# Cross-attention mix from split float32r operands, with new rings and queue orders, in a one-core post-norm decoder layer

## Chip, cores and metric

One core of one Trainium2 chip runs the whole layer. The metric is the device time of one execution in microseconds (us). Before the change it is 554.73 us, the median of three runs (554.62 to 554.76).

## The reference

The input x has 8 sequences of 112 tokens and 1024 features, the context 8 x 375 tokens x 1024. All is float32.

```python
x = layernorm(x + self_attention(x))        # 16 heads of 64, rotary, causal; Wq, Wk, Wv, Wo of 1024x1024
a = einsum('bqd,bkd->bqk', x, ctx)          # cross-attention, one head of 1024 features
e = softmax(a, axis=-1)
c = einsum('bqk,bkd->bqd', e, ctx)          # the "mix"
x = layernorm(x + c)
y = x @ weight.T + bias + lora(x)           # 1024x1024; adapters of rank 16, by batch
x = layernorm(x + y)
```

## The kernel before

The layer is one program for TensorE (PE), ScalarE (ACT), VectorE (DVE), GpSimd (POOL) and SyncE (SP). Each engine has an order of calls written out by hand, and semaphores join them: an engine does nothing else while one of its instructions waits.

**Split products.** Nearly all matrix products are made of three float32r matmuls: an operand is rounded to float32r by ACT (`hi`), the rest `raw - hi` is kept as a second float32r operand (`lo`), and hi·hi + hi·lo + lo·hi is summed in PSUM. The rests of weights and context are made by POOL, those of activations by DVE. The one large product that is not split is `cross_mix` (L658 to L673): it multiplies plain float32 tiles, `cprob_t` (the exponentials, turned by PE) by `ctx_tok` (the context by tokens, 125 tokens x 1024 in each of three tiles). Each of its six matmuls per batch stands in the trace as two records.

**Stages.** First the value and the query/key projections with self-attention (to about 280 us). Then the stage that the change is about, in which three things are woven together on PE, from about 305 us to the end:

- `wo(i, n)`: token tile i (128 tokens, 7 tiles) times half n of Wo, 24 matmuls of 512 columns (L573). DVE adds the residue, POOL takes the power -1/2 of the variance (`power`, L1416 and L1419), ACT normalises (`norm_x1`), PE turns the tile (`turn_tile`, L619), ACT and DVE round it and form its rest.
- cross-attention of batch b (8 batches): `cross_score(b)`, 24 matmuls of 376 columns (L644) against the context by features, `cf_hi` and `cf_lo`, in four chunks of two feature tiles (L334 loads a chunk, L904 rounds it on ACT, L1409 makes its rest on POOL); the maximum (DVE) and exponential (ACT); `turn_cprob(b)` (L656); `keep_cprob_t(b)` (ACT); `cross_mix(b)`; `add_row(b)` (DVE, L1259), `power(1, b)` (POOL), `norm_x2(b)` (ACT, L914) and `turn_row(b)` (PE, L630).
- `ffn(i, n)`: tile i times half n of the feed-forward weight, again 24 matmuls at L573, then two more with the low-rank part and the bias (L606, L608). For n = 0 `low_rank(i)` stands within it (L684 to L689); its result is masked by DVE (`mask_t`). Half n needs all eight blocks of weight n: loaded by `load_ff(u)` (L358), rounded by ACT (`round_ff`), rests by POOL (`rest_ff`, L1432). Blocks 0 to 3 and 12 to 15 first get the identity added by POOL (`add_one`, L1427).

**Context buffers.** The four chunks of `cf` have a place each; chunk j of the next batch is loaded once chunk j of this one has been scored. The three tiles of `ctx_tok` (L342, L343) are loaded again once the mix of the batch before has used them, and ACT and POOL have no work with them.

**PE's order** around the mix, as an example: `turn_cprob(1), turn_row(0), wo(6, 0), cross_mix(1), turn_tile(3), cross_score(2), wo(4, 1), turn_cprob(2), turn_row(1), wo(5, 1), cross_mix(2)`. The feed-forward calls come in the order (0,0), (1,0), (2,0), (0,1), (1,1), (2,1), and then tile by tile. All loads go through SP's queue, in one written order; a load whose wait is not met holds back those behind it.

## Time and profile before

| | us |
|---|---|
| median of 3 runs | 554.73 |
| profiled execution, own time | 555.06 |
| its span, first to last instruction | 553.2 |
| PE busy | 545.4 (99%) |
| DVE / ACT / POOL busy | 203.8 / 214.0 / 201.3 |

The span is the time from the first to the last instruction of the profiled execution; its own time holds 1.86 us around that. An engine is busy while it executes, not while it waits. The chain of waits is followed back from the last instruction: it names what the end really hung on at each moment.

### The profile page before, as it was taken

Reading aid. Unit: us, or ns where it says so; the run is one execution under the profiler, and the core shown is the slowest. Engines: PE = TensorE matmul, PEld = TensorE weight load, DVE = VectorE, ACT = ScalarE, POOL = GpSimd, SP = SyncE. Lnnn points to the kernel's source line nnn. Section 1 sums busy time; section 2 is a strip of 40 time slices with the busy share of each in tenths; the row PEclk is TensorE's granted clock in tenths of the full one; section 3 lists DMA queues with packets and bytes.
Section 4 is the critical chain, followed back from the end, with each engine's and each line's share of the span. In section 5 each row is a group of like instructions: output and inputs, shape, how many; then the busy total and the mean of one; then the engine's idle time right before and its main releaser. Section 6 shows DMA issues by size and latency. Waiting matters only on the chain.

```text
span 553.2 us, 7743 instructions
## 1 busy us (share of the span) xinstructions
PE 545.4 (99%) x2998; PEld 451.1 (82%) x2998; DVE 203.8 (37%) x474; ACT 214.0 (39%) x521; POOL 201.3 (36%) x171
## 2 busy tenths in 40 slices
PE   8999999999999999999999999999999999999995
PEld 6888889988889888888888887778778687877784
DVE  5810000243434435252544643334434423233321
ACT  5703201053645353452536353234553551622221
POOL 0004401533355555541003665143974771600100
PEclk9999999999999999999999999999999999999999
DMA  9906521621111111100077735869737745451001
GB/s 286 296 1 183 162 56 57 197 71 39 39 39 40 39 40 39 38 2 2 1 217 199 188 109 155 244 182 281 229 115 231 206 127 143 171 169 40 4 35 76
DMA packets 36916, 65.66 MB, mean 119 GB/s; under 512 B 3832, under 2 KB 19448, under 8 KB 36880
## 3 DMA queue, kind: packets, MB, share of 16 engines
q1 hardware_dynamic: 36352, 64.91, 40.1%
q8 instruction: 24, 0.39, 0.3%
q10 hardware_dynamic: 528, 0.26, 0.2%
q14 instruction: 12, 0.10, 0.1%
HBM read 54.14 MB, written 3.67 MB: 105 GB/s over the span
## 4 chain that ended last, share of the span: by engine, by line
PE 99%; DVE 0%; ACT 0%; POOL 0%; issue 0%; POOLq 0%
PE bank L450 29%; PE bank L573 28%; PE bank L461 14%; PE bank L669 7%; PE bank L644 6%; PE bank L475 3%; PE bank L502 3%; PE bank L489 2%; PE bank L630 1%; PE bank L619 1%; PE bank L533 1%; PE bank L689 1%; PE bank L606 1%; PE bank L686 1%; PE bank L608 1%; PE bank L656 0%
## 5 line engine op out<-in xcount | busy, mean ns | idle before, releaser
L450 PE MATMUL bank<-x_hi,w_hi 128*128 128x448 f32 x256 | 96.5, 377 | 0.0
L450 PE MATMUL bank<-x_hi,w_lo 128*128 128x448 f32 x256 | 93.9, 367 | 0.0
L450 PE MATMUL bank<-x_lo,w_hi 128*128 128x448 f32 x256 | 93.9, 367 | 0.0
L1396 POOL TENSOR_TENSOR w_lo<-w_mix,w_hi 128x1024 fp32r<-128x1024 f32 x16 | 40.5, 2530 | 116.7 <-ACT w_hi L808 116.7
L573 PE MATMUL bank<-ffn,act_hi 128*128 128x512 f32 x224 | 70.9, 398 | 0.0
L573 PE MATMUL bank<-wo,act_hi 128*128 128x512 f32 x224 | 70.2, 394 | 0.0
L1409 POOL TENSOR_TENSOR cf_lo<-cf_raw,cf_hi 128x752 fp32r<-128x752 f32 x32 | 56.9, 1804 | 33.7 <-ACT cf_hi L904 33.7
L823 ACT ACTIVATE prob<-prob,shift 112x112 f32<-112x112 f32 x128 | 47.9, 375 | 48.3 <-DVE shift L1158 48.3
L450 PEld LDWEIGHTS bank<-x_hi,w_hi 128*128 128x128 f32 x256 | 48.1, 188 | 5.5
L450 PEld LDWEIGHTS bank<-x_hi,w_lo 128*128 128x128 f32 x256 | 48.0, 188 | 4.5
L450 PEld LDWEIGHTS bank<-x_lo,w_hi 128*128 128x128 f32 x256 | 48.2, 188 | 3.9
L1137 DVE TENSOR_TENSOR q_feat<-bank,turn 128x448 f32<-128x448 f32 x16 | 10.0, 625 | 111.9 <-PE bank L450 111.9
L573 PEld LDWEIGHTS bank<-ffn,act_hi 128*128 128x128 f32 x224 | 41.1, 188 | 8.6 <-issue 1.0
L573 PEld LDWEIGHTS bank<-wo,act_hi 128*128 128x128 f32 x224 | 41.2, 188 | 8.4
L1416 POOL TENSOR_TENSOR norm<-norm,minus_half 128x1 f32<-128x1 f32 (+1 forms) x22 | 12.1, 551 | 98.1 <-DVE norm L1214 98.1
L573 PE MATMUL bank<-ffn,act_lo 128*128 128x512 f32 x112 | 43.7, 391 | 0.0
L573 PE MATMUL bank<-wo,act_lo 128*128 128x512 f32 x112 | 43.7, 390 | 0.0
L669 PE MATMUL bank<-ctx_tok,cprob_t 125*112 125x512 f32 x96 | 42.6, 593 | 0.0
L1385 POOL TENSOR_TENSOR w_mix<-w_raw 128x512 f32<-128x512 f32 x16 | 20.6, 1288 | 48.9 <-DMA w_raw<-qkv_w 47.5
L1402 POOL TENSOR_TENSOR wo<-half_raw,wo 128x512 fp32r<-128x512 f32 x16 | 20.7, 1317 | 41.8 <-ACT wo L867 41.8
L461 PE MATMUL bank<-wv_hi,x_hi 128*128 128x512 f32 x112 | 35.9, 390 | 0.0
L461 PE MATMUL bank<-wv_lo,x_hi 128*128 128x512 f32 x112 | 35.8, 389 | 0.0
(108 smaller groups left out, 898.0 us busy)
## 6 DMA issues: line engine op xcount, KB each, us to landing
cf_raw<-ctx_feat SPq DMA_DIRECT2D x32, 376.0 KB, 5.2
ctx_tok<-ctx_tok SPq DMA_DIRECT2D x24, 448.0 KB
w_raw<-qkv_w SPq DMA_DIRECT2D x16, 512.0 KB, 3.4
half_raw<-wo_w SPq DMA_DIRECT2D x16, 256.0 KB, 5.6
...
out<-y_t SPq DMA_DIRECT2D x6, 512.0 KB, 2.7
```

What stands on the lines that cost most here:

```text
L450: last = pe.matmul(to[:, 0:HT], a[:, k, :], b[:, k, HT * h:HT * h + HT], start=(k == 0 and b is x_hi and a is w_hi[w]), stop=(k == KT - 1 ...
L461: return pe.matmul(value_bank(c, i)[:, :], a[:, k, tile_of(i)], w[c][:, k, :], start=(k == 0 and a is x_hi and w is wv_hi), stop=(k == KT ...
L475: last = pe.matmul(SCORE[h][0:S, b * S:(b + 1) * S], qk[u][0][rows, HB * r + b, :], qk[u][1][rows, HB * r + b, :], start=True, stop=True)
L502: last = pe.matmul(heads_bank(p, r)[HD * h:HD * h + HD, (b - HB * r) * S:(b - HB * r + 1) * S], v[:, HD * h:HD * h + HD], prob_t[2 * r + h ...
L573: last = pe.matmul(to[:, :], a[:, k, cols], weight(of, n, k, w), start=(k == 0 and a is act_hi and w == 0), stop=(ends and k == KT - 1 and ...
L644: last = pe.matmul(CSCORE[0:S, 0:LKP], a[:, k, tokens_of(b)], c[:, k, :], start=(k == 0 and a is act_hi and c is cf_hi), stop=(k == KT - 1 ...
L669: last = pe.matmul(MIX[n][0:S, :], cprob_t[:, c, :], ct[c][:, HALF * n:HALF * n + HALF], start=(c == 0), stop=(c == CC - 1))
L823: last = act.activation(prob[a][:, b, :], prob[a][:, b, :], ACT.Exp, bias=shift[:, a, b:b + 1], scale=SCORE_SCALE, accum_out=total[:, a, b ...
L1385: pool.tensor_tensor(mix[:, :, 0, :], raw[:, :, 0, :], raw[:, :, 1, :], ALU.add)
L1396: pool.tensor_tensor(w_lo[w][:, :, :], w_mix[:, :, :], w_hi[w][:, :, :].bitcast(F32), ALU.subtract).then_inc(w_rest, 1)
L1402: pool.tensor_tensor(half_w[0][n][:, at_q, 1, :], half_raw[n][:, at_q, 1, :], half_w[0][n][:, at_q, 0, :].bitcast(F32), ALU.subtract).then ...
L1409: pool.tensor_tensor(cf_lo[:, CK * j:CK * j + CK, :], cf_raw[:, CK * j:CK * j + CK, :], cf_hi[:, CK * j:CK * j + CK, :].bitcast(F32), ALU. ...
```

## The change

**The mix.** `cross_mix` now multiplies `cprob_hi`, `cprob_lo` by `ct_hi`, `ct_lo`: three float32r matmuls for each of six halves (3 token tiles x 2 column halves, now half by half: all three tiles for n = 0, then for n = 1). Half m = 6b + 3n + c.

- ACT: `keep_cprob_t` writes `cprob_hi` in float32r; 48 new `round_ct(m)` (125x512) write `ct_hi`, a ring of five places, so that half m may be rounded only when half m - 5 has been multiplied. Places 2 to 4 of the ring lie where the fourth chunk of `cf` was.
- POOL: 48 new `rest_ct(m)` write `ct_lo` over `ct_raw`.
- DVE: 8 new `rest_cprob_t(b)` (125x336). (A `rest_ct` is also defined for DVE, and not called.)

**Chunks of cf** keep their size (two feature tiles) but rotate over three places after the first four: chunk m may be loaded once chunk m - 3 is scored. `cross_score(b)` is called in two parts: chunks 0 to 2 right after `turn_cprob(b - 1)`, chunk 3 just ahead of `cross_mix(b - 1)`.

**Small ones.** The low-rank operand `a_both` has 112 columns instead of 128, and is loaded in runs of 448 bytes; `t_both` becomes a ring of three tiles, so `mask_t(i)` waits for `ffn(i - 3, 1)` from i = 3; some small tiles move.

**Orders.** PE, after `turn_tile(1)`: score(0), wo(4,0), turn_cprob(0), turn_tile(2), score(1) 0-2, wo(5,0), score(1) 3, mix(0), wo(3,1), turn_cprob(1), score(2) 0-2, turn_row(0), wo(6,0), score(2) 3, mix(1), turn_tile(3), wo(4,1), turn_cprob(2), score(3) 0-2, turn_row(1), wo(5,1), score(3) 3, mix(2), turn_tile(4), wo(6,1), turn_cprob(3), score(4) 0-2, turn_row(2), ffn(0,0), score(4) 3, mix(3), turn_tile(5), ffn(1,0), turn_cprob(4), score(5) 0-2, turn_row(3), **ffn(0,1)**, score(5) 3, mix(4), turn_tile(6), ffn(1,1), turn_cprob(5), score(6) 0-2, turn_row(4), ffn(2,0), score(6) 3, mix(5), ffn(2,1), and so on; ffn(0,1) comes ahead of mix(4) and of ffn(2,0). It is given as a diff at its first place:

```diff
+            first, last = range(3), range(3, 4)
             turn_tile(2)
+            cross_score(1, first)
             wo(5, 0)
+            cross_score(1, last)
             cross_mix(0)
-            cross_score(1)
             wo(3, 1)
```

POOL, from `rest_ct(11)` to `rest_ff(15)`: add_one 0, 1; ff 0, 1; add_one 2; cf 14; power(1,1); ff 2; ct 12 to 16; cf 15; power(0,4); add_one 3; cf 16; ff 3; ct 17; cf 17; ff 4, 5; cf 18; power(1,2); ff 6, 7; ct 18 to 21; cf 19; ct 22; power(0,5); ff 8, 9; ct 23; ff 10; cf 20; ff 11; add_one 12; cf 21; ff 12; add_one 13, 14; cf 22; ff 13; power(1,3); ff 14; add_one 15; ct 24; ff 15.

SP, from mix(1) on: ff 0, 1, 2; cf 14; ff 3 to 7; ct(2) in three tiles; cf 15, 16, 17; row(4, 0); cf 18; row(4, 1); ct(3); ff 8 to 11; cf 19; ff 12; cf 20; ff 13; cf 21; ff 14, 15. ACT has, between mix(1) and turn_row(1): round_ct(11), cross_exp(2), round_ff(0), (1), round_turned(a3), round_cf(14), round_ff(2), round_ct(12), norm_x2(1), round_ct(13), (14), (15), keep_cprob_t(2), round_ct(16), round_turned(b1), round_cf(15).

The core of the diff:

```diff
+HALVES = 2 * CC
+CT_HI = 5
+T_RING = 3
...
+        cf_at = [X0 + 32768 + 6016 * i for i in range(4)]
+        cf_hi = [at(f"cf_hi{i}", [P, CK, LKP], where, F32R) for i, where in enumerate(cf_at)]
...
+        ct_raw = [at(f"ct_raw{c}", [CR, D], S0 + 4096 * c) for c in range(CC)]
+        ct_lo = [at(f"ct_lo{c}", [CR, D], S0 + 4096 * c, F32R) for c in range(CC)]
+        ct_hi = [at(f"ct_hi{i}", [CR, HALF], where, F32R)
+                 for i, where in enumerate([S0 + 25600, S0 + 27648]
+                                           + [cf_at[3] + 2048 * i for i in range(3)])]
...
+        def cf_slot(m):
+            return (m, 1) if m < 4 else ((m - 4) % 3, (m - 4) // 3 + 2)
+        def cf_before(m):
+            return m - 3 if m < 7 else m - 2
...
             def load_cf(m):
                 b, j = divmod(m, CJ)
+                slot, _ = cf_slot(m)
                 if b:
-                    sp.wait_ge(cscored, CJ * (b - 1) + j + 1)
+                    sp.wait_ge(cscored, cf_before(m))
...
+            def load_ct(b, c):
+                if b:
+                    sp.wait_ge(ct_used, HALVES * (b - 1) + CC + c + 1)
...
-                for c in range(CC):
-                    pe.wait_ge(ct_in[c], 32 * (b + 1))
-                    for n in range(2):
-                        last = pe.matmul(MIX[n][0:S, :], cprob_t[:, c, :],
-                                         ct[c][:, HALF * n:HALF * n + HALF],
-                                         start=(c == 0), stop=(c == CC - 1))
-                    last.then_inc(ct_used, 1)
+                for n in range(2):
+                    for c in range(CC):
+                        m = HALVES * b + CC * n + c
+                        cols = slice(HALF * n, HALF * n + HALF)
+                        hi = ct_hi[m % CT_HI]
+                        pe.wait_ge(ct_rest[n], CC * b + c + 1)
+                        pe.matmul(MIX[n][0:S, :], cprob_hi[:, c, :], hi[:, :],
+                                  start=(c == 0), stop=False)
+                        pe.matmul(MIX[n][0:S, :], cprob_hi[:, c, :], ct_lo[c][:, cols],
+                                  start=False, stop=False)
+                        pe.wait_ge(cprob_rest, b + 1)
+                        pe.matmul(MIX[n][0:S, :], cprob_lo[:, c, :], hi[:, :],
+                                  start=False, stop=(c == CC - 1)).then_inc(ct_used, 1)
...
+            def round_ct(m):
+                b, r = divmod(m, HALVES)
+                n, c = divmod(r, CC)
+                act.wait_ge(ct_in[c], 32 * b + 32)
+                if m in (2, 3, 4):
+                    act.wait_ge(cscored, CJ)
+                if m >= CT_HI:
+                    act.wait_ge(ct_used, m - CT_HI + 1)
+                act.activation(ct_hi[m % CT_HI][:, :], ct_raw[c][:, HALF * n:HALF * n + HALF],
+                               ACT.Copy).then_inc(ct_rounded, 1)
...
+            def rest_cprob_t(b):
+                dve.wait_ge(cprob_t_kept, b + 1)
+                dve.tensor_tensor(cprob_lo[:, :, :],
+                                  CTURN[0:CR, 0:CC * S].rearrange("p (c s) -> p c s", c=CC),
+                                  cprob_hi[:, :, :].bitcast(F32), ALU.subtract).then_inc(cprob_rest, 1)
...
+            def rest_ct(m):
+                b, r = divmod(m, HALVES)
+                n, c = divmod(r, CC)
+                cols = slice(HALF * n, HALF * n + HALF)
+                pool.wait_ge(ct_rounded, m + 1)
+                pool.tensor_tensor(ct_lo[c][:, cols], ct_raw[c][:, cols],
+                                   ct_hi[m % CT_HI][:, :].bitcast(F32),
+                                   ALU.subtract).then_inc(ct_rest[n], 1)
```

## Rows read from the trace of the kernel before

**Rows 1.** The page: busy time of each engine, and the chain's shares.
```profile
PE 545.4 (99%) x2998; PEld 451.1 (82%) x2998; DVE 203.8 (37%) x474; ACT 214.0 (39%) x521; POOL 201.3 (36%) x171
...
PE 99%; DVE 0%; ACT 0%; POOL 0%; issue 0%; POOLq 0%
```

**Rows 2.** The chain in order of time: start us, us, what.
```profile
320.79 0.87 PE bank L619 x8
...
344.29 5.15 PE bank L669 x12
349.44 4.12 PE bank L644 x24
353.56 5.46 PE bank L573 x24
359.02 0.32 PE bank L656 x3
359.34 0.77 PE bank L630 x8
...
411.36 0.12 issue
411.48 0.47 PE bank L606
...
430.76 5.38 PE bank L669 x12
...
519.72 2.04 PE bank L573 x9
...
527.04 0.77 PE bank L630 x8
...
546.69 0.24 PE bank L608
```

**Rows 3.** Groups by line, 300 to 553 us: xcount, busy us, mean ns, idle before.
```profile
L1409 POOL TENSOR_TENSOR cf_lo<-cf_raw,cf_hi 128x752 fp32r<-128x752 f32 x32 | 56.9, 1804 | 33.7 <-ACT cf_hi L904 33.7
L1432 POOL TENSOR_TENSOR ffn<-half_raw,ffn 128x512 fp32r<-128x512 f32 x16 | 20.2, 1291 | 1.9 <-ACT ffn L946 1.9
...
L946 ACT ACTIVATE ffn<-half_raw 128x512 fp32r<-128x512 f32 x16 | 8.7, 616 | 3.3 <-POOL half_raw L1427 3.3
...
L1237 DVE TENSOR_TENSOR act_lo<-bank,act_hi 128x448 fp32r<-128x448 f32 x16 | 9.2, 614 | 0.0
```

**Rows 4.** POOL's instructions in order of time: start, us, what, [idle before].
```profile
374.14 0.55 POOL L1416 TENSOR_TENSOR norm<-norm,minus_half 112x1 f32<-112x1 f32 x1 [5.53 <-DVE norm L1214]
374.77 0.20 POOL L1419 TENSOR_TENSOR norm<-norm 112x1 f32<-112x1 f32 x1
...
390.80 1.70 POOL L1427 TENSOR_TENSOR half_raw<-half_raw,ident 128x128 f32<-128x128 f32 x4
...
429.71 7.01 POOL L1409 TENSOR_TENSOR cf_lo<-cf_raw,cf_hi 128x752 fp32r<-128x752 f32 x4 [1.29 <-ACT cf_hi L904]
...
441.68 5.03 POOL L1432 TENSOR_TENSOR ffn<-half_raw,ffn 128x512 fp32r<-128x512 f32 x4
```

**Rows 5.** SP's issues and ACT's first use of a chunk, in order of time.
```profile
365.63 1.77 SPq L358 DMA_DIRECT2D half_raw<-ffn_w  x4
...
372.68 3.41 SPq L334 DMA_DIRECT2D cf_raw<-ctx_feat  x4
...
379.98 1.75 ACT L904 ACTIVATE cf_hi<-cf_raw 128x752 fp32r<-128x752 f32 x2 [2.07 <-DMA cf_raw<-ctx_feat]
```

**Rows 6.** DMA by stretches (us from start, length, clock, share, GB/s).
```profile
370.00:374.00 4.00, 1.00 0.97 245
374.00:378.00 4.00, 1.00 1.03 230
378.00:382.00 4.00, 1.00 1.04 362
382.00:386.00 4.00, 1.00 1.04 286
```

**Rows 7.** DMA issues: KB each, median us to landing.
```profile
b_raw<-ffn_w SPq DMA_DIRECT2D x1, 512.0 KB, 9.4
...
ident<-identity SPq DMA_DIRECT2D x1, 64.0 KB, 3.7
...
mask<-causal SPq DMA_DIRECT2D x1, 49.0 KB, 3.4
```

**Rows 8.** ACT in order of time: the first norm_x1 and the first norm_x2.
```profile
318.24 1.25 ACT L909 ACTIVATE x_t<-x_t,norm 128x1024 f32<-128x1024 f32 x1 [8.80 <-POOL norm L1419]
...
353.57 1.25 ACT L914 ACTIVATE row<-row,norm 112x1024 f32<-112x1024 f32 x1 [12.64 <-POOL norm L1419]
```

**Rows 9.** POOL's busy time in one stretch (start, length, busy, clock, DMA share, GB/s).
```profile
371.00:431.00 60.00, 36.41 (x37) 1.00 0.72 207
```

**Rows 10.** The tile cf_raw: time of its 32 loads, and ACT's rounding of it.
```profile
L904 ACT ACTIVATE cf_hi<-cf_raw x32: 813/828/856, 306.5 to 479.0; 128x752 fp32r<-128x752 f32 x32
...
DMA to landing us min/median/max: 3.1/5.2/12.8
```

More of the change, by code:

```diff
@@ L1477, in _ @@
[L1477 to L1478 removed]
+            rest_ct(11)
+            add_one(0)
+            add_one(1)
             rest_ff(0)
             rest_ff(1)
[L1481 to L1492 removed]
@@ L1493, in _ @@
-            for u in range(8, 12):
-                rest_ff(u)
-            for m in range(20, 24):
-                rest_cf(m)
-            for u in range(12, 16):
-                add_one(u)
+            add_one(2)
+            rest_cf(14)
+            power(1, 1, S)
+            rest_ff(2)
+            rest_ct(12)
+            rest_ct(13)
+            rest_ct(14)
+            rest_ct(15)
+            rest_ct(16)
+            rest_cf(15)
+            power(0, 4, P)
+            add_one(3)
+            rest_cf(16)
@@ new lines, in _ @@
+            rest_ff(3)
+            rest_ct(17)
+            rest_cf(17)
+            rest_ff(4)
+            rest_ff(5)
+            rest_cf(18)
+            power(1, 2, S)
+            rest_ff(6)
+            rest_ff(7)
+            rest_ct(18)
+            rest_ct(19)
+            rest_ct(20)
+            rest_ct(21)
+            rest_cf(19)
+            rest_ct(22)
+            power(0, 5, P)
+            rest_ff(8)
+            rest_ff(9)
+            rest_ct(23)
+            rest_ff(10)
+            rest_cf(20)
@@ new lines, in _ @@
+            rest_ff(11)
+            add_one(12)
+            rest_cf(21)
+            rest_ff(12)
+            add_one(13)
+            add_one(14)
+            rest_cf(22)
+            rest_ff(13)
+            power(1, 3, S)
+            rest_ff(14)
+            add_one(15)
+            rest_ct(24)
+            rest_ff(15)
+            rest_ct(25)
+            rest_cf(23)
+            rest_ct(26)
+            rest_ct(27)
+            rest_ct(28)
+            power(0, 6, P)
+            rest_cf(24)
@@ L1499, in _ @@
+            rest_ct(29)
+            rest_cf(25)
+            rest_cf(26)
+            rest_ct(30)
             power(1, 4, S)
-            for u in range(12, 16):
-                rest_ff(u)
-            for m in range(24, 28):
-                rest_cf(m)
+            rest_ct(31)
+            rest_ct(32)
+            rest_ct(33)
+            rest_ct(34)
             power(2, 0, P)
-            power(1, 5, S)
+            power(2, 1, P)
+            rest_cf(27)
             rest_cf(28)
             rest_cf(29)
-            power(2, 1, P)
+            rest_ct(35)
```

533 lines of the change are left out of this document (334 added, 199 removed).

## The prediction

> **What bounds the kernel now.** I read the page first: PE is busy for 99% of the span, and 99% of the chain that ended last is PE [rows 1]. The chain in order of time then shows the stage of the change as one unbroken row of PE pieces, each beginning where the one before ends, from the first turn at 320.79 to the last matmul, which ends at 546.93 [rows 2]. Every other engine has been late only once or twice: 0.12 + (0.47 - 0.23) = 0.36 us ahead of L606, and 0.23 us in the one mix that took 5.38 instead of 5.15 [rows 2]. So PE's work is the time, to the microsecond, and POOL, ACT and DVE are hidden, at 36 to 39% of the span [rows 1]. The question is whether they stay so.
>
> **PE's work.** One mix takes 5.15 us [rows 2]. Split, it is 6 x 3 = 18 float32r matmuls of 512 columns; 24 such take 5.46 us [rows 2], 0.228 each, so a mix takes 18 x 0.228 = 4.10. The rows with 125 context tokens in place of 128 and 112 output columns in place of 128 are not measured for this form; the scores, with 112 columns, run at 4.12/24 = 0.172 for 376 columns [rows 2], which is what the width alone makes of 0.228 (0.168), so I take no surcharge. Bounds: 0.228, and 0.286, at which the split mix costs what the old one did. Saving: 8 x 1.05 = 8.4 us. With 112 columns in `a_both` the 56 matmuls that load all of it save at most what a turn of 112 saves against one of 128, (0.87 - 0.77)/8 = 0.0125 each [rows 2], 0.7 us; half of that change lies on the moving side, so I take 0.3 (bounds 0 and 0.7). The two small stalls of 0.36 and 0.23 belong to the old order; I let them go (0.6). Sum: 8.4 + 0.3 + 0.6 = 9.3 us. The profiled execution of 555.06 would become 545.8; the median of the runs lies 0.33 lower, so 545.4 if PE never waits.
>
> **POOL.** It gains 48 `rest_ct` of 125x512; the rest of a weight block, 128x512, is the same work on 2% more rows: 1.29 us alone, 5.03/4 = 1.26 back to back [rows 3, 4]. That is 48 x 1.26 = 60 us on top of what it does in this stage. ACT gains 48 x 0.616 = 30 us less overlap [rows 3], DVE eight subtractions no longer than 0.614 [rows 3], 5 us; both have more than half of the stage free, and I cost these at nothing as long as their order doesn't hold a rounding behind a load.
>
> POOL's load isn't even. I laid out PE's new order from 320.79 with the pieces of [rows 2] (turn of a tile 0.87, of a row 0.77, of the exponentials 0.32, three quarters of a score 3.09, one quarter 1.03, wo 5.46, ffn with n = 0 7.3 (519.72 to 527.04), mix 4.10): mix(1) starts at 368.7, mix(2) at 389.8, ffn(0,0) at 404.4, mix(3) at 412.7, ffn(0,1) at 429.2. The last is the tight one: ffn(0,1) needs all eight blocks of the second weight half, so POOL must have passed `rest_ff(15)`. POOL can't be ahead at the start of that stretch: `rest_ct(11)` waits for the ring of five, that is for the first half of mix(1), 368.7 + 0.7 = 369.4, plus rounding 0.6 and itself 1.26: 371.4. Behind it stand, up to and with `rest_ff(15)`: 9 chunks of cf at 7.01/4 = 1.76 (15.8), 13 rests of ct and 16 of weights at 1.26 (36.5), 8 add_one at 1.70/4 = 0.42 (3.4), 5 power at 0.55 + 0.20 and a gap, 0.78 (3.9) [rows 4]. Sum 59.6 us: 431.0, against 429.2. So PE waits at least 1.8 us even if POOL never does.
>
> And POOL will wait, for DMA. SP issues eight weight blocks (2.1 MB) and a chunk of cf from wo(6,0)'s end at 367.7, ahead of ct(2). Before, with a nearly equal queue, four blocks, three ctx tiles and a chunk, the blocks issued at 365.6 and the chunk landed at 379.98 [rows 5], at 230 to 362 GB/s with all DMA engines busy [rows 6]. Now x_t(6), a piece of row 3, eight blocks, a chunk and the first tile of ct(2) stand there, 3.8 MB; from 367.4 at the mean of those four stretches, 281 GB/s, the last lands at 380.8; at the slowest, 230, at 383.9. `rest_ct(12)` then starts 0.7 later, at 381.5, where POOL was done with `rest_ff(2)` at about 379.4: 2 us idle, and 0.3 to 0.5 more for each of the next two tiles. So POOL's column is late by about 3 us, and passes `rest_ff(15)` at 434 to 434.5 instead of 431.0.
>
> On PE this comes out piece by piece, as lateness against the plan:
> - `turn_row(1)`, due 382.5, waits for `norm_x2(1)`, which ACT has behind `round_ct(12)`: 380.8 + 0.6 + 1.25 [rows 8] = 382.7. 0 to 1.4 us, I take 0.3.
> - score(3)'s last chunk, due 388.8, needs `rest_cf(15)`, which POOL has behind `rest_ct(12)` to `(16)`: from 381.5 at least 5 x 1.26 + 0.5 idle + 1.76 = 390.1. Lateness 1.3.
> - the last half of mix(2), due 3.4 after its first, needs `rest_ct(17)`, behind power, add_one, chunk 16 and `rest_ff(3)`: 390.1 + 0.78 + 0.42 + 1.76 + 1.26 + 1.26 = 395.6, where PE is there at 394.6. Another 1.0; lateness 2.3.
> - `turn_row(3)` needs power(1,3) and `norm_x2(3)`, some 0.8 late; then ffn(0,1) starts at 434.3 instead of 429.2. Lateness 5.1, and this holds all of those before it.
> Behind ffn(0,1) POOL has 6 ct, 3 to 4 cf and one power per mix, 14 us in a period of 22, so the lateness doesn't grow, but for 0.2 to 0.4 in the sixth half of some mixes. I take 5.5 in all: 545.4 + 5.5 = 550.9 us. Own bounds 548.5 (1.8 of POOL's sum, 1.3 for loads) and 553.
>
> **Other edits.** Score in two parts adds waits, no work. Chunk 3 of the next batch may be loaded only after its chunk 0 is scored, 7.5 us before it is due in the wo part; landing 3.1 at best and 5.2 in the median [rows 10], rounding 0.83 [rows 10] and rest 1.8 [rows 3] take 5.7 to 7.8; the queue is nearly empty at that moment, so I take the lower end and nothing, and at the upper end it is 0.3 us a batch. `norm_x1(0)` now stands behind `round_low` on ACT, and so behind the landing of b_raw, 307.9 + 9.4 = 317.3 [rows 7], plus 1.0: 318.3, against 318.24 before [rows 8] and a turn at 320.79: nothing, with 1.2 us of cover. `turn_row(0)`, due 361.4, has `norm_x2(0)` behind three tiles of ct(1): about 360.7, cover 0.6. The ring of `t_both` waits for work that is 40 us old.
>
> **Two rules of the Trainium skill.** The weight rest of 128x512 takes 1.26 to 1.29 us on POOL [rows 3, 4]. The Trainium skill's page "GPSIMD Engine Reference", section "Performance versus the Vector engine", gives about 2.6 cycles per element for two inputs and counts GpSimd as about half as fast as VectorE for such work; 512 x 2.6 / 1.2 GHz is 1.11 us, an estimate by that page. By it the 29 rests of the stretch would be 4 us shorter and POOL's sum would end at 427, ahead of PE; the measured row decides here, and the page's advice speaks against putting 60 us more on this engine. The loads with runs of 448 bytes don't look dear: 49 KB in such runs landed in 3.4 us and 64 KB in runs of 512 in 3.7 [rows 7]. The Trainium skill's page "DMA: Bandwidth & Descriptors", in its opening table, wants 512 bytes at least, and has a read-modify-write below; were a_raw to take twice as long, `norm_x1(0)` would lose its 1.2 us of cover and little more.
>
> **Rivals.**
> - *PE never waits much*: POOL and the loads keep up but for the 1.8 us. For it: before, POOL was busy for 36.4 of the 60 us from 371 to 431 [rows 9], and the last chunks of a load burst came at 362 GB/s [rows 6]. Against: the sum of 59.6 is of rows. 545.4 to 548.5, say 547.2.
> - *The loads come late*: at 230 GB/s everything behind ct(2) shifts by 3 us more. 545.4 + 8.3 = 553.7. For it: the stretch that was slow before held just these blocks [rows 6].
> - *Slower, by the ring of five*: the sixth half of every mix may be rounded only 0.7 us into it, and PE wants it at 3.4. With 0.6 for rounding and 1.26 for the rest, 0.8 us are to spare. If POOL stands in a run of two chunks of cf (3.5 us) when it comes, PE waits 2.7, with one chunk 1.0; four mixes of each kind make 14.8, and 545.4 + 14.8 = 560.2. It decides from 9.3/8 = 1.2 us a mix. Against: POOL's order has at most one chunk and one block ahead of `rest_ct(6b + 5)`.
> - *The split mix is no faster*, for its 125 rows or for operands that PE takes slower: 8.4 us of the saving go, 559.
>
> **How the numbers follow.** Forecast 0.47, 550.9. PE never waits much 0.22. Late loads 0.17. Ring 0.09. No faster mix 0.05. The predicted time is 550.9. Two in ten are left out by a range from 546.3 to 555.0: it cuts a little of the second case and all of the last two. What can be told from no change is 0.2%, 1.1 us: faster is under 553.6, that is the first two cases and some 0.11 of the third: 0.80. Same is 553.6 to 555.8: the rest of the third and a little of the others, 0.08. Slower 0.12.
>
> **What would show it.** L669's successor at 0.228 a matmul and 4.10 a mix, or the first step is wrong. POOL without a gap from about 382 to about 434, ending in `rest_ff(15)`, and PE's largest wait just ahead of ffn(0,1), on it. Waits before that on the chunk of score(3) and on the last half of mix(2). ACT waiting for a landing at `round_ct(12)` near 380.8. If POOL has gaps all through that stretch and PE none, the time is near 546; if ACT's `round_ct` are late at every mix's sixth half, the ring decides.

## The result, and the profile after

The changed kernel takes 558.9 us, the median of four runs (558.8 to 560.49), where the kernel before took 554.75 (554.62 to 554.8). The ratio is 1.0076 [1.0055, 1.0098]: slower, by four microseconds, where 550.9 was forecast and 546.3 to 555.0 given as the range. The profiled execution took 558.8, with a span of 557.0.

The page, of the kernel after: busy time, granted clock of TensorE in tenths, and the shares of the chain, which answer to [rows 1].

```profile
PE 541.4 (97%) x3046; PEld 461.1 (83%) x3046; DVE 207.2 (37%) x482; ACT 241.5 (43%) x569; POOL 262.1 (47%) x219
...
PEclk9999999999999999999999999999899799999999
...
PE 85%; DMA 6%; POOL 3%; issue 2%; ACT 2%; SPq 1%; DVE 1%; POOLq 0%; ACTq 0%; DVEq 0%
```

PE held 99% of the chain before; it now holds 85%, and the rest goes through loads, POOL and ACT. That row is the first sign that PE's work is no longer the time. The clock row has an 8 and a 7 in it.

What PE waited for after 300 us, by the waits of PE (engine, line, releaser: us in total, times, longest). Of the kernel before the same view has no row at all.

```profile
PE bank L710 <- POOL cf_lo L1587: 2.4, 1, 2.4
PE bank L694 <- ACT row L1008: 2.2, 2, 1.9
PE bank L637 <- issue: 1.6, 1, 1.6
PE bank L757 <- DVE cprob_lo L1426: 1.3, 1, 1.3
PE bank L739 <- POOL ct_lo L1596: 0.4, 1, 0.4
PE bank L670 <- DVE t_both L1454: 0.3, 1, 0.3
```

PE in order of time where the two longest stand (start, us, what, idle before); L710 is the score, L739 and L741 the mix, L694 `turn_row`, L637 `wo` and `ffn`.

```profile
391.35 0.45 PE L710 MATMUL bank<-cf_hi,act_hi 128*112 128x376 f32 x1 [2.38 <-POOL cf_lo L1587]
...
393.16 0.63 PE L739 MATMUL bank<-ct_hi,cprob_hi 125*112 125x512 f32 x1
393.59 0.63 PE L741 MATMUL bank<-ct_lo,cprob_hi 125*112 125x512 f32 x1
...
395.38 0.40 PE L739 MATMUL bank<-ct_hi,cprob_hi 125*112 125x512 f32 x1
395.62 0.39 PE L741 MATMUL bank<-ct_lo,cprob_hi 125*112 125x512 f32 x1
...
435.34 1.25 PE L694 MATMUL bank<-ident,row 112*128 112x112 f32 x8 [1.90 <-ACT row L1008]
438.22 1.19 PE L637 MATMUL bank<-ffn,act_hi 128*128 128x512 f32 x2 [1.63 <-issue]
```

The starts of the mix are 0.43 us apart right after the wait (393.16, 393.59) and 0.24 two microseconds later (395.38, 395.62). The same work costs 1.8 times the time. The windows tell why (start, length, busy time of PE, PEld, DVE, ACT, POOL, granted clock, DMA share, GB/s; the first answers to [rows 9]).

```profile
371.00:431.00 60.00, 57.23 (x302) 48.21 (x301) 27.46 (x68) 37.42 (x64) 52.94 (x50) 0.97 0.74 218
...
392.00:396.00 4.00, 4.00 (x14) 3.27 (x13) 0.77 (x3) 3.02 (x5) 3.94 (x4) 0.63 0.40 118
396.00:400.00 4.00, 4.00 (x24) 3.23 (x23) 1.48 (x3) 3.81 (x8) 4.00 (x4) 1.00 0.61 170
...
436.00:440.00 4.00, 2.37 (x8) 1.75 (x7) 1.16 (x2) 2.83 (x6) 4.00 (x4) 0.50 0.40 128
440.00:444.00 4.00, 4.00 (x13) 3.16 (x12) 0.00 (x0) 0.00 (x0) 4.00 (x4) 0.66 0.00 0
```

Behind these waits the granted clock stands at its lower level, 1.2 GHz of 2.4, for a few microseconds (0.63 and 0.50, then 0.66), and returns to 1.00 while PE works.

**The account.** I cut PE's trace into its calls by the start times of the matmuls and compared each with the median of its kind over three kernels (the changed kernel, which is called after from here on, and the two versions h_dve and i_dve below): 24 matmuls of `wo` 5.55, three quarters of a score 3.15, a mix 4.16, and so on. The excess over these is PE's lateness, with a wait booked on the call ahead of it. From 319 us to the end it is 13.4 us. The table has its large parts, which add up to 13.6; many small differences of the other calls take off the rest.

| where | late, us | of it low clock |
|---|---|---|
| `turn_row(0)` | 0.5 | |
| `wo(5,1)`, waiting for score(3)'s last chunk | 2.5 | |
| that chunk and mix(2) | 1.6 | 1.6 |
| mix(3), its last half | 0.65 | |
| ahead of `turn_row(3)` | 2.1 | |
| `turn_row(3)`, waiting for ffn(0,1) | 2.2 | 0.5 |
| ffn(0,1) | 2.1 | 2.1 |
| ffn(2,0), on `mask_t` | 0.5 | |
| ahead of `low_rank(4)` | 1.5 | |

On the other side, eight mixes of 5.15 became eight of 4.16 (7.9), `low_rank` went from 1.32 to 1.23 seven times (0.6), the exponentials' turn from 0.31 to 0.25 eight times (0.5), and the old stalls went (0.6). 13.4 - 9.6 = 3.8, and the spans differ by 557.0 - 553.2 = 3.8. So the question is where the 13.4 come from; 4.2 of them are low clock.

**POOL's column**, the waits of POOL from 369 to 438.2:

```profile
POOL ct_lo L1596 <- ACT ct_hi L998: 2.6, 3, 0.9
POOL cf_lo L1587 <- ACT cf_hi L986: 2.2, 1, 2.2
POOL half_raw L1614 <- DMA half_raw<-ffn_w: 1.2, 2, 1.0
POOL ffn L1619 <- ACT ffn L1040: 0.6, 1, 0.6
```

and POOL in order of time at four of the places that matter (L1596 is `rest_ct`, L1587 `rest_cf`, L1619 `rest_ff`):

```profile
381.39 1.29 POOL L1596 TENSOR_TENSOR ct_lo<-ct_raw,ct_hi 125x512 fp32r<-125x512 f32 x1 [0.90 <-ACT ct_hi L998]
...
389.43 1.77 POOL L1587 TENSOR_TENSOR cf_lo<-cf_raw,cf_hi 128x752 fp32r<-128x752 f32 x1
...
428.05 1.29 POOL L1619 TENSOR_TENSOR ffn<-half_raw,ffn 128x512 fp32r<-128x512 f32 x1 [0.64 <-ACT ffn L1040]
...
436.84 1.27 POOL L1619 TENSOR_TENSOR ffn<-half_raw,ffn 128x512 fp32r<-128x512 f32 x1
```

The first half of ct(2) came at 381.39, `rest_cf(15)` at 389.43 behind five halves, and the block that ends at 438.11, `rest_ff(15)`, let ffn(0,1) go at 438.22. The chain of waits around the first of these (start, us, what) reads the same way, from a load to PE:

```profile
374.67 10.27 DMA ct_raw<-ctx_tok
...
384.96 0.64 ACT ct_hi L998
...
385.67 3.80 POOL ct_lo L1596 x3
389.47 1.74 POOL cf_lo L1587
391.21 0.14 issue
391.35 2.02 PE bank L710 x6
```

### The profile page after: what moved, and what is told of

The parts are those of the page before. It is cut to its first block, busy times and chain, and to the rows that moved or that the text cites. A ratio compares the mean times of both kernels' runs of the same rounds, so it can differ in the third digit from the quotient of the medians.

```text
span 557.0 us, 7996 instructions
## 1 busy us (share of the span) xinstructions
PE 541.4 (97%) x3046; PEld 461.1 (83%) x3046; DVE 207.2 (37%) x482; ACT 241.5 (43%) x569; POOL 262.1 (47%) x219
## 4 chain that ended last, share of the span: by engine, by line
PE 85%; DMA 6%; POOL 3%; issue 2%; ACT 2%; SPq 1%; DVE 1%; POOLq 0%; ACTq 0%; DVEq 0%
PE bank L514 29%; PE bank L637 21%; PE bank L525 14%; DMA ct_raw<-ctx_tok 6%; PE bank L710 4%; PE bank L539 3%; PE bank L566 3%; PE bank L553 2%; PE bank L739 2%; PE bank L741 2%; PE bank L744 2%; POOL ct_lo L1596 1%; PE bank L597 1%; PE bank L694 1%; PE bank L683 1%
## 5 line engine op out<-in xcount | busy, mean ns | idle before, releaser
L1596 POOL TENSOR_TENSOR ct_lo<-ct_raw,ct_hi 125x512 fp32r<-125x512 f32 x48 | 61.4, 1292 | 33.8 <-ACT ct_hi L998 33.7
L637 PE MATMUL bank<-ffn,act_hi 128*128 128x512 f32 x224 | 72.0, 403 | 1.6 <-issue 1.6
L637 PE MATMUL bank<-wo,act_hi 128*128 128x512 f32 x224 | 70.3, 395 | 0.0
L1587 POOL TENSOR_TENSOR cf_lo<-cf_raw,cf_hi 128x752 fp32r<-128x752 f32 x32 | 57.9, 1826 | 7.8 <-ACT cf_hi L986 7.8
L998 ACT ACTIVATE ct_hi<-ct_raw 125x512 fp32r<-125x512 f32 x48 | 29.4, 627 | 49.8 <-DMA ct_raw<-ctx_tok 38.9
L637 PEld LDWEIGHTS bank<-ffn,act_hi 128*128 128x128 f32 x224 | 42.0, 193 | 10.3 <-issue 1.9
L637 PEld LDWEIGHTS bank<-wo,act_hi 128*128 128x128 f32 x224 | 41.2, 188 | 8.5
L637 PE MATMUL bank<-ffn,act_lo 128*128 128x512 f32 x112 | 44.5, 397 | 0.0
L637 PE MATMUL bank<-wo,act_lo 128*128 128x512 f32 x112 | 43.7, 390 | 0.0
```

The costliest lines, as they stand in the source:

```text
L637: last = pe.matmul(to[:, :], a[:, k, cols], weight(of, n, k, w), start=(k == 0 and a is act_hi and w == 0), stop=(ends and k == KT - 1 and ...
L998: act.activation(ct_hi[m % CT_HI][:, :], ct_raw[c][:, HALF * n:HALF * n + HALF], ACT.Copy).then_inc(ct_rounded, 1)
L1587: pool.tensor_tensor(cf_lo[slot][:, :, :], cf_raw[slot][:, :, :], cf_hi[slot][:, :, :].bitcast(F32), ALU.subtract).then_inc(cf_rest, 1)
L1596: pool.tensor_tensor(ct_lo[c][:, cols], ct_raw[c][:, cols], ct_hi[m % CT_HI][:, :].bitcast(F32), ALU.subtract).then_inc(ct_rest[n], 1)
```

## The experiments

Each ratio is against runs of the kernel before on the same chip, whose median lay between 555.2 and 555.6; ratios are compared, not times. Edits are to the changed kernel unless another is named.

**e4_nosplit and e7_nosplit_blocks: the orders without the split.** In e4 the mix is plain float32 again, and `round_ct`, `rest_ct` and their waits are gone; rings, loads and orders are those after. In e7, the same kernel, the blocks 12 to 15 are also rounded and rested sooner, and get their identity sooner.

```diff
-            pe.wait_ge(ct_rest[n], CC * b + c + 1)
-            (three matmuls of ct_hi, ct_lo)
+            pe.wait_ge(ct_in[c], 32 * (b + 1))
+            pe.matmul(MIX[n][0:S, :], cprob_hi[:, c, :], ct_raw[c][:, cols], ...)
```
```diff
 ACT (e7)                        POOL (e7)
+ round_ff(12)                   + add_one(13), (14), (15)
+ round_ff(13), (14), (15)         rest_cf(21)
  keep_t_part(1)                   rest_ff(12)
- round_ff(12) ... round_ff(15)  - add_one(13) ... (15)
```

> The changed kernel with its orders, rings and loads, but the mix from plain float32 operands again (six matmuls per batch, no round_ct, no rest_ct). Theory (roundings and rests of the context are what TensorE waits for): 545.4 without waits plus the 8.4 us of the float32 mix, 553.8, and at most 1 us of waits: 554.5. Rival (the new orders and the rotating chunks cost by themselves): 557 or more, with waits ahead of score or turn_row as in the changed kernel.

> The same edit of order on the kernel with plain float32 mix (no round_ct, no rest_ct), which took 558.35 us. There GpSimd has 10 us of gaps between 405 and 436, so its column isn't full. Theory A: the hang of blocks 12 to 15 on low_rank(1) was its whole bind; the waits ahead of turn_row(3) (1.1) and ffn(0,1) (2.1) and the low clock behind them (1.6) go: 553.6 us. Rival (loads of the blocks land too late in the new order of SyncE, whatever ScalarE does): waits ahead of ffn(0,1) as before, 558.

e4: 558.35, ratio 1.0055 [1.0034, 1.0075]. My theory (without POOL's added work the time returns to that of before) was wrong: with 48 rests fewer the kernel is still slower than before. The lateness falls from 13.4 to 6.6 us, but the old mix costs 7.9 more on PE. POOL in order of time, e4:

```profile
426.68 1.29 POOL L1566 TENSOR_TENSOR ffn<-half_raw,ffn 128x512 fp32r<-128x512 f32 x1 [3.12 <-ACT ffn L1035]
...
435.59 1.27 POOL L1566 TENSOR_TENSOR ffn<-half_raw,ffn 128x512 fp32r<-128x512 f32 x1 [1.34 <-ACT ffn L1035]
```

POOL is idle for 3.12 us and still late. `rest_ff(12)` waits for `round_ff(12)`, which ACT has behind `keep_t_part(1)`, and that is the result of `low_rank(1)`, inside ffn(1,0). ACT's row of `keep_t_part(1)` in e4:

```profile
425.81 0.27 ACT L1050 ACTIVATE t_part<-bank 48x128 f32<-48x128 f32 x1 [2.66 <-PE bank L757]
```

So in e4 the last four blocks can't start before PE is one call from needing them. Of its 6.6 us of lateness 4.7 lie from ahead of `turn_row(3)` to the end of ffn(0,1). e7 breaks that tie: 553.66, 0.9961 [0.9946, 0.9976], as expected to 0.1 us, lateness 1.3. Orders and rings are cheap then; in the kernel without the split this tie cost 5 us.

**e6_blocks: the same order edit with the split mix.** POOL also does `rest_ct(24)` behind `rest_ff(15)` here instead of ahead of it.

> The changed kernel with one edit of order: ScalarE rounds weight blocks 12 to 15 ahead of keep_t_part(1) and of norm_x2(3), and GpSimd does add_one 13 to 15 right behind rest_ff(11) and rest_ff(15) ahead of rest_ct(24). Theory A (two binds, each enough: GpSimd's column is full from 413 to 438 us, and beside it blocks 12 to 15 hang on low_rank(1) over ScalarE's order): only rest_ct(24) is taken out of the column, so ffn(0,1) starts 1.3 us earlier, 437 instead of 438.2, and the time is 557.5. Rival B (the order of ScalarE alone held GpSimd up): ffn(0,1) starts at 434 or earlier, about 554.

555.59, 1.0000 [0.9984, 1.0015]: 4.2 us better than after, between the two expectations. Lateness 9.8. `rest_ff(15)` ends at 436.0 instead of 438.1, and 1.3 of these 2.1 us are `rest_ct(24)`, which no longer stands ahead of it. ffn(0,1) waits for 0.2 only and PE keeps its clock there (2.6 us of low clock go), but mix(4) waits now (1.3), since the halves 24 to 28 stand behind the blocks, and ffn(1,0) waits for its `mask_t` (1.7). With POOL full, moving one thing forward moves another back.

**e1_ct_first and e10_cf15: loads.** e1 issues the tiles of ct(2) ahead of blocks 3 to 7; e10 also has the chunks 15 to 17 between blocks 5 to 7, and `rest_cf(15)` ahead of `rest_ct(15)`.

```diff
 SP (e1)             SP and POOL (e10)
+ load_ct(2, 0..2)   + load_ct(2, 0..2)
  load_ff(3..7)        load_ff(3), (4)
- load_ct(2, 0..2)   + load_cf(15), load_ff(5), load_cf(16), ...
                     + rest_cf(15)
                       rest_ct(15), (16)
                     - rest_cf(15)
```

> The changed kernel with one edit: the three context tiles of batch 2 are issued ahead of weight blocks 3 to 7 instead of behind them. Theory (late tiles, then a full GpSimd): the tiles are rounded at about 376 to 380 us instead of 380.7, 382.8 and 385.0; TensorE no longer waits ahead of the last chunk of score(3) (2.6 us, plus 1.6 us at the low clock behind it). GpSimd's column behind them is still full, so ffn(0,1) starts at about 435 instead of 438.2, still after a wait and at the low clock. About 556 us against 558.9. Rival (GpSimd's work alone sets it, the loads are hidden): the same within 0.5 us, 558.5. Rival (the low clock is a thing by itself and no result of the waits): the clock row shows 0.63 near 392 to 396 as before.

> e1_ct_first with the weight blocks 5, 6, 7 issued between chunks 15, 16, 17, and rest_cf(15) ahead of rest_ct(15) and (16). Theory (score(3)'s last chunk was held twice, by its landing and by GpSimd's order): no wait ahead of it and no low clock at mix(2), so 555.9 - 1.3 - 1.0 = 553.6; the waits ahead of turn_row(3) and ffn(0,1) stay as they are or grow by part of it, GpSimd's column being full. Rival (GpSimd's column is what sets ffn(0,1), and every microsecond won ahead of it is lost in waiting there): 555.5.

e1: 555.87, 1.0017 [0.9997, 1.0036], as expected: 3.3 us come back, and the windows from 388 to 400 show a clock of 1.00. But score(3) still waits 1.2, because `round_cf(15)` now stands behind the blocks (it waits for its load until 388.25), and mix(2) and mix(3) wait for their sixth halves (0.9 and 1.7 late). e10 removes that wait altogether and is no better, 558.11, 1.0053 [1.0035, 1.0070]: a miss by 4.5 us. Its profiled execution, the shortest of its five (556.17), has 1.7 of lateness in mix(2), on `rest_ct(17)`, 1.5 in mix(3), and 5.6 from ahead of `turn_row(3)` to the end of ffn(0,1), where after has 6.4. The time at which ffn(0,1) may start hangs on the blocks, so most of what is won ahead of it is waited out there. In the profiled executions of after, e1, e3, e4, e6 and e10 it starts at 438.2, 437.9, 439.4, 437.0, 436.1 and 436.7, each time 0.1 us behind the end of `rest_ff(15)`.

**e3_filler: the clock by itself.** Nine more matmuls of 512 columns at each of three places of the long waits. Their result lies in a bank that the next mix starts anew, so nothing is left out or changed but PE's occupation.

```diff
             wo(5, 1)
+            fill(2, 9)
             cross_score(3, last)
...
+            fill(4, 9)
             turn_row(3)
+            fill(4, 9)
             ffn(0, 1)
```

> The changed kernel with three runs of 9 matmuls of 512 columns (2.05 us each), whose results are overwritten, put where TensorE now waits: ahead of the last chunk of score(3), ahead of turn_row(3) and ahead of ffn(0,1). Theory (the low clock follows from the waits): the granted clock stays at 1.00, nothing runs at the lower level; of the 4.3 us that the low clock costs nearly all come back: 554.8 us, 555.5 if the filler overruns the waits by 0.7. Rival (the clock falls for another reason): clock rows as before, 559 to 561.

556.65, 1.0021 [1.0009, 1.0033]. 27 matmuls more, 6.2 us of work, make the kernel 3 us faster than after, where 4.1 were expected. The window of e3 that answers to the 0.50 above:

```profile
436.00:440.00 4.00, 4.00 (x23) 2.83 (x22) 1.15 (x2) 3.90 (x7) 4.00 (x5) 1.00 0.61 201
```

The clock stays at 1.00 in this and the other five windows that I read (388 to 400, 432 to 444), and ffn(0,1) loses nothing to it. The blocks came no sooner: `rest_ff(15)` ends at 439.25, 1.1 us later than in after, and mix(2) waits 0.9 us for its sixth half. So the 4.2 us of low clock went, and about one came back as waits. This shows the term; it is no way to write kernels, since a shorter wait gives the same and more.

**e2_dve_rests: 18 of the rests on DVE.** `rest_ct(12)` to `(29)` by VectorE, 23 us off POOL.

> The changed kernel with the 18 rests of the context halves of batches 2, 3 and 4 on VectorE instead of GpSimd, loads as in the changed kernel. Theory (GpSimd's column is over-full): GpSimd sheds 18 x 1.26 = 23 us, passes rest_ff(15) over 6 us earlier, and TensorE waits neither ahead of turn_row(3) nor ahead of ffn(0,1): 2.1 + 2.1 us and 2.7 us of low clock go. The chunk of score(3) is still about 1.6 us late, for the tiles land as late as before. About 552 us. Rival (the loads alone): over 557. Rival (VectorE and GpSimd get in each other's way, each of them reading two operands from SBUF): the rests on VectorE take well over the 0.69 us of the same operation early in the kernel, or GpSimd's over 1.3.

559.99, 1.0071 [1.0047, 1.0095]: a miss by 8 us. The tile `ct_lo` on DVE (ns, min/median/max):

```profile
L1435 DVE TENSOR_TENSOR ct_lo<-ct_raw,ct_hi x18: 677/693/2325, 383.5 to 450.9; 125x512 fp32r<-125x512 f32 x18
```

DVE does one in 0.69 us, half of POOL's 1.29. But some take 2.3, and POOL's rests take 1.73 and 2.25 in places instead of 1.27 and 1.80. The cause shows best in h_dve, first POOL's row and then DVE's:

```profile
418.65 1.83 POOL L1593 TENSOR_TENSOR cf_lo<-cf_raw,cf_hi 128x752 fp32r<-128x752 f32 x1
```
```profile
418.68 2.35 DVE L1435 TENSOR_TENSOR ct_lo<-ct_raw,ct_hi 125x512 fp32r<-125x512 f32 x1 [0.69 <-ACT ct_hi L998]
```

DVE started 0.03 us behind POOL and ended at 421.03, 0.55 behind POOL's end at 420.48. Alone it takes 0.68, so it had done next to nothing when POOL was done. The Trainium skill, on its page "SBUF — State Buffer", section "Who interferes with whom", says that a DVE instruction with two SBUF inputs takes the second through the read interface that it shares with GpSimd, and that the shared ports are an exclusive lock. The trace agrees: 2.35 us beside a POOL instruction of 1.83. The other reason for the miss is that relieving POOL does nothing for blocks that wait on ACT: POOL waits 2.7 us for `round_ff(12)` in e2. And ACT was late itself, since a DVE behind POOL made the maximum of score(4) late (ACT waits 2.9 us for it). PE lost 7.4 us from ahead of `turn_row(3)` to ffn(0,1).

**e8_tail and e9_tail2: the last batches.** ACT takes `keep_cprob_t(7)`, `keep_y(3,1)`, `norm_x2(6)` and `keep_t_part(4)` ahead of `round_ct(44)` to `(46)`, for the wait at `low_rank(4)`. In e9 `round_ct(47)` also comes ahead of `norm_y(3)`.

```diff
+ keep_cprob_t(7)
  round_ct(43)
+ keep_y(3, 1), norm_x2(6), keep_t_part(4)
  round_ct(44), (45), (46)
- keep_cprob_t(7) ... keep_t_part(4)
- norm_y(3)                      (e9)
  round_turned("b6"), round_ct(47)
+ norm_y(3)                      (e9)
```

> The changed kernel with one edit of ScalarE's order: keep_cprob_t(7), keep_y(3,1), norm_x2(6) and keep_t_part(4) ahead of the roundings that wait for the last two tiles of batch 7. Theory: the wait of 1.55 us ahead of low_rank(4) goes and none takes its place, for nothing is late behind it: 557.4 against 558.9. Rival (the wait moves into ffn(4,0) or mix(7), whose tiles are no earlier): 558.5 or more.

> e8_tail, mended: round_ct(47) is put ahead of norm_y(3). Theory: what made e8_tail slower than the changed kernel was that mix(7) waited 4.1 us for round_ct(47), and 2.1 us of low clock behind; that goes, and the wait of 1.55 ahead of low_rank(4) stays away: 561.7 - 4.1 - 2.1 = 555.5 to 557.4. Rival (e8_tail was slow for its chip): 560.

e8: 561.7, 1.0113 [1.0090, 1.0136], 2 us slower than after instead of 1.5 faster. The wait at `low_rank(4)` is gone, and mix(7) is 4.1 us late with 2.1 of low clock behind it. The same order is in g_dve below (where e8 has a wait of 3.65 us it has 3.63), and ACT reads there:

```profile
506.79 1.24 ACT L1072 ACTIVATE y_t<-y_t,norm 128x1024 f32<-128x1024 f32 x1 [3.63 <-POOL norm L1612]
...
509.40 0.64 ACT L998 ACTIVATE ct_hi<-ct_raw 125x512 fp32r<-125x512 f32 x1
```

`norm_y(3)` waits 3.63 us for a power that POOL has behind the rests 44 to 46, and half 47, which PE wants, stands behind it. I had moved ACT's work without asking what the instruction that now comes first waits for. e9: 557.41, 1.0042 [1.0027, 1.0058], within its expectation, and no wait in the tail.

**f_pool, f_dve, g_dve, g_pool, h_dve: the edits together.** f_pool is e1 and e6 with `norm_x2` ahead of the round before it in five batches, and half 23, `keep_t_part(2)` and `keep_cprob_t(7)` earlier. f_dve is f_pool with `rest_ct(18)` to `(23)` on DVE. g_dve interleaves the loads as e10 and has e8's tail, and `keep_t_part(1)` and `rest_ct(29)` one place earlier; g_pool is g_dve without DVE. h_dve mends g_dve by e9's order, `rest_cf(15)` ahead of `rest_ct(15)`, and half 23 earlier on ACT and DVE.

```diff
 DVE (f_dve)                    POOL (h_dve)
  rest_turned("a4")               rest_ct(14)
+ rest_ct(18), (19)             + rest_cf(15)
  add_wo(13)                      rest_ct(15), (16)
+ rest_ct(20), (21), (22)       - rest_cf(15)
  rest_cprob_t(3)
  ...
+ rest_ct(23)
```

> Repairs together, all rests still on GpSimd: context tiles of batch 2 loaded first, blocks 12 to 15 as in e6_blocks, norm_x2 of batches 0, 1, 2, 4, 5 ahead of the rounding that waits for the last tiles, rest_ct(23) ahead of rest_ff(9), keep_cprob_t(7) ahead of round_ct(43). Theory (GpSimd's work against TensorE's plan: 59.6 us against 57.8 at least 1.8 late): one wait of 2 to 4 us ahead of ffn(0,1) stays, with low clock behind it; the 1.55 us ahead of low_rank(4) and the small waits go. 551 us, 549 to 553. Rival (waits move elsewhere): 554 and more.

> As f_pool, with the six rests of batch 3 (rest_ct 18 to 23) on VectorE, 7.6 us off GpSimd's column ahead of ffn(0,1). Theory: GpSimd passes rest_ff(15) ahead of TensorE, no wait over 1 us is left anywhere and the clock stays at 1.00: 548 us, 546.5 to 550. VectorE's rests take 0.69 us when GpSimd is idle and up to 2.3 when it is not, as in e2_dve_rests, where GpSimd's own rose too. Rival (this mutual hold costs what the shift gives): 551 or more.

> f_dve with the waits that its trace still shows taken up one by one: weight blocks 5, 6, 7 are issued between the chunks 15, 16, 17 of the context instead of ahead of them (in f_dve ScalarE waited until 387.97 for chunk 15, issued at 380.56 behind five blocks, and TensorE waited 2.2 us and ran 1.0 us longer at the low clock); keep_t_part(1) ahead of round_ct(25) (0.8 us); rest_ct(29) ahead of rest_cf(24) (1.2 us); and ahead of the last context tiles ScalarE does keep_y(3,1), norm_x2(6) and keep_t_part(4) (1.6 us). Theory (waits on queue order and on landings, and the clock behind them, are all that stands between the kernel and its sum): 551.9 - 2.2 - 1.0 - 0.8 - 1.2 - 1.6 = 545.1, with some rest of waits 546 us, 545 to 548. Rival (every wait taken away comes back at the next place, the loads together being too many): 550 or more.

> The same edits as g_dve with all rests on GpSimd. Theory (GpSimd's 59.6 us ahead of ffn(0,1) against 57.8 of TensorE): waits of 2 to 3 us between ffn(1,0) and mix(4) stay, the others go: 549 us. Rival (GpSimd's work fits after all, only the orders were wrong): as g_dve, 546.

> g_dve with its three remaining waits taken up: round_ct(47) ahead of norm_y(3) (in g_dve mix(7) waited 3.5 us, and the low clock behind it cost 1.6), rest_cf(15) ahead of rest_ct(15) and (16) on GpSimd (1.8 us and 1.0 of low clock), and rest_ct(23) ahead of the chunk and the statistics that held it (1.4). Theory (each long wait is one place in an in-order queue, and costs its length and the low clock behind it): 554.0 - 9.3 = 544.7 at best, 547 with what is left; 545.5 to 549. Rival (the waits come back elsewhere): 551 or more.

| | median | ratio | lateness of PE |
|---|---|---|---|
| f_pool | 554.99 | 0.9981 [0.9967, 0.9995] | 10.5 |
| f_dve | 551.93 | 0.9924 [0.9906, 0.9943] | 6.0 |
| g_dve | 554.0 | 0.9979 [0.9962, 0.9996] | 8.7 |
| g_pool | 557.03 | 1.0037 [1.0022, 1.0053] | 11.8 |
| h_dve | 551.23 | 0.9930 [0.9912, 0.9949] | 4.8 |

All five were forecast too fast, by 4 to 8 us, since each time I had counted the waits that went and not those that came. Six rests on DVE are worth 3 us in each pair (f, g), where 18 were worth less than nothing: these six stand where POOL has the blocks 8 to 11 to do as well; that this is the reason is argued, not shown. f_dve still has 2.1 ahead of score(3): its chunk 15 was loaded behind blocks 3 to 7, and ACT waited for it:

```profile
387.97 0.83 ACT L986 ACTIVATE cf_hi<-cf_raw 128x752 fp32r<-128x752 f32 x1 [2.52 <-DMA cf_raw<-ctx_feat]
```

h_dve has only one long wait, 3.1 us in mix(2):

```profile
397.50 0.49 PE L739 MATMUL bank<-ct_hi,cprob_hi 125*112 125x512 f32 x1 [3.08 <-POOL ct_lo L1602]
```

That is the sixth half, 17, which the ring of five lets ACT round only when the first half of mix(2) is multiplied, and which ACT then had behind `norm_x1(4)` and a block, and POOL behind a power, an `add_one`, a chunk and a block.

The same wait had been there before, and was misread. The expectations of e10, g_dve and h_dve book about 1.0 us at mix(2) as low clock. But in e1, f_dve and g_dve PE's clock is 1.00 there, and the mix is 0.9 late in one place, ahead of its sixth half, where two matmuls start 1.04 us apart instead of 0.23. In f_dve (the wait, one of two, then the clock):

```profile
PE bank L739 <- POOL ct_lo L1602: 1.5, 2, 0.8
392.00:396.00 4.00, 3.54 (x16) 2.34 (x14) 0.77 (x3) 4.00 (x9) 4.00 (x3) 1.00 0.60 156
396.00:400.00 4.00, 3.82 (x21) 3.22 (x22) 2.64 (x5) 2.84 (x6) 4.00 (x4) 1.00 0.95 260
```

So the edits that were to take the clock away left this wait, and let it grow when PE came sooner: 1.7 late in e10, 3.35 in h_dve.

**i_dve and e11_ct17: one half moved.** The same edit on h_dve and on e10.

```diff
 ACT                    POOL
+ round_ct(17)            power(0, 4)
  norm_x1(4)            + rest_ct(17)
  round_ff(3)             add_one(3)
- round_ct(17)            rest_cf(16), rest_ff(3)
                        - rest_ct(17)
```

> The version h_dve with one half-tile moved in both queues: ScalarE rounds half 17 (the sixth of mix(2)) ahead of norm_x1(4) instead of behind it and a weight block, and GpSimd makes its rest right behind the power for tile 4 instead of behind add_one(3), rest_cf(16) and rest_ff(3). In h_dve the mix(2) took 7.51 us instead of 4.15, and rest_ct(17) ended at 397.4 with PE there at 394.2. Theory (what is left is the order around the ring of five, the prediction's third rival): the rest ends at about 394.1, the wait of 3.4 goes and 0 to 0.5 comes back later, since GpSimd does the same work in the same time: 0.9930 becomes 0.987 to 0.988 of the kernel before, 548 us where before is 555.2. Rival (GpSimd's sum is the limit in this stretch, whatever its order): chunk 16, weight block 3 and what follows are 1.3 us later, the wait comes back ahead of score(4), turn_row(2) or ffn(0,0): 550.5 us or more.

> The same move of half 17 put on e10_cf15, whose profiled execution had a wait of 1.4 us in mix(2) for rest_ct(17), 2.0 with a low clock at turn_row(3) and 2.1 + 1.6 around ffn(0,1). Theory: 1.4 us go and GpSimd's later work in the column to rest_ff(15) stays where it is, so PE arrives 1.4 us sooner at a ffn(0,1) that is not ready sooner, and waits there instead: 557.5 to 558.1 with e10_cf15 at 558.1 in its job (ratio 1.004 to 1.005). Rival (each wait is a cost of its own): 556.5 or less, ratio under 1.003.

i_dve: 548.1 us (547.39 to 548.74), ratio 0.9870 [0.9856, 0.9884], as expected. It beats both kernels, the one before by 7.1 us. PE's waits after 300 us are down to two rows, and POOL makes the rest in time:

```profile
PE bank L694 <- ACT row L1008: 1.8, 2, 1.2
PE bank L637 <- issue: 0.2, 1, 0.2
```
```profile
390.95 0.56 POOL L1609 TENSOR_TENSOR norm<-norm,minus_half 128x1 f32<-128x1 f32 x1
...
391.73 1.29 POOL L1602 TENSOR_TENSOR ct_lo<-ct_raw,ct_hi 125x512 fp32r<-125x512 f32 x1
```

The lateness is 2.8. Of the 3.4 us that went, 1.7 came back ahead of `turn_row(2)`, which the rival had for all of it; the rest stayed won. e11: 555.55, 1.0005 [0.9992, 1.0018], against e10's 1.0053. Here the rival was right by the measured ratios. The profiled execution of e11, though, is the longest of its twelve (558.02; the shortest took 553.51), and shows what the theory said: no wait in mix(2), 2.6 ahead of `turn_row(2)` and 7.1 from ahead of `turn_row(3)` to the end of ffn(0,1). Which of the two happens in the shorter executions no trace here shows.

## Why the forecast was wrong, step by step

- **The saving on PE was right.** The mix takes 4.16 where 4.10 was said (7.9 us saved of 8.4), `low_rank` gained 0.6 for 0.3, the exponentials' turn 0.5 for nothing, and the two old stalls went. The span less the lateness is 557.0 - 13.4 = 543.6, with 1.8 around it 545.4, the number forecast for a PE that never waits. "No faster mix" is out.
- **POOL's work was right**: `rest_ct(11)` ended at 371.5 (371.4 was said), and the column to `rest_ff(15)` is 438.1 - 371.5 = 66.6 less 6.6 of waits, 60.0, against 59.6.
- **The failed step: "POOL's column is late by about 3 us, and passes `rest_ff(15)` at 434 to 434.5".** It passed at 438.1, having waited 6.6, and ffn(0,1) started at 438.22 where 434.3 was said. The three landings of ct(2) cost what was forecast (2.6 in all, and the first rest at 381.39 for 381.5), so late loads of ct(2), the second rival, are out; the parts differ, since `rest_ff(2)` ended at 380.5 and not at "about 379.4", which is 379.0 by the forecast's own terms. Not in the sum were 1.2 for the blocks' own landing at `add_one(0)`, 2.2 for chunk 19, whose load stands behind the blocks 8 to 11 and the tiles of ct(3), and 0.6 for ACT's order at `rest_ff(12)`. ACT had been put at nothing "as long as their order doesn't hold a rounding behind a load", and at `rest_ff(12)` it does (below). I had asked what POOL was full with, not what each of its instructions waited for on ACT and SP. No run takes the waits for chunk 19 and for `add_one(0)` away by themselves, so what each is worth on PE is not shown.
- **ACT's order at the last blocks.** In after `round_ff(12)` stands behind `keep_t_part(1)`, and both behind `round_ct(25)`, whose tile landed only at 426.5; PE was past `low_rank(1)` at 425.95:

```profile
426.52 0.63 ACT L998 ACTIVATE ct_hi<-ct_raw 125x512 fp32r<-125x512 f32 x1 [1.58 <-DMA ct_raw<-ctx_tok]
427.18 0.27 ACT L1055 ACTIVATE t_part<-bank 48x128 f32<-48x128 f32 x1
427.35 0.62 ACT L1040 ACTIVATE ffn<-half_raw 128x512 fp32r<-128x512 f32 x1
```

  In e4, without `round_ct`, the same order waits for `low_rank(1)` itself. There it alone holds the blocks back (3.1 and 1.3 of idle POOL), and breaking it is worth 0.0094 of the time, 5 us. With the split the edit is worth 4, of which the tie, 0.6 in POOL's row, is only a part: the rest is `rest_ct(24)` moved out of the way and the clock that no longer falls.
- **Lateness isn't the sum of waits.** The step took the waits as 0.3, 1.3, 1.0, 0.8 and so on, and no clock. The measured waits at score(3) and ffn(0,1) are 2.5 and 1.7 to 2.2, and behind them PE ran at its lower level: 1.6 us lost in score(3) and mix(2), 2.6 in `turn_row(3)` and ffn(0,1). e3 confirms this term by itself: with PE kept busy the clock stays at 1.00.
- **Behind the start of ffn(0,1)** the lateness grew by 4.1, where 0.4 was allowed for: 2.1 of low clock, 0.5 at `mask_t` in ffn(2,0), 1.5 at `low_rank(4)`, whose PSUM bank is free only when ACT and DVE have made `cprob_hi` and `cprob_lo`; ACT had that behind two roundings of ct(7), which waited for their loads. PSUM, the memory of banks that PE writes its sums to, wasn't in the forecast at all.
- **The ring of five**, the rival for slower, didn't decide the time after: its mechanism costs 0.65 there, at mix(3). It was real all the same: mix(2) is 0.9 late by it in e1, e3, f_dve and g_dve, and waits 1.4 in e10 and 3.1 in h_dve, once the earlier waits are gone, against the 1.0 and 2.7 worked out for it. Taking it away in mix(2) is the one edit from h_dve to i_dve, and took 3.3 us off.
- **The small ones.** `turn_row(0)` had a cover of 0.6 and was 0.5 late, with `norm_x2(0)` behind a landing. The 448-byte runs show no cost: a_raw landed in 7.8 us, and in 8.4 before with more bytes.

In place of 5.5 the lateness was 13.4. Against the forecast's plan ffn(0,1) started 9.0 late (438.22 for 429.2, where 5.1 was said), and 4.1 came behind it; this adds up to 13.1, 0.3 less than the account, because the plan's pieces aren't quite the measured ones. By kind it was 9.2 of waits and 4.2 of clock. What remains open: which of e11's waits its shorter executions lack, what the waits for chunk 19 and `add_one(0)` are worth by themselves, and when a wait costs the clock (below).
